# One attention and RWKV-style channel-mix block: row sums in the exp, a reordered layer norm, stores on another queue, and an add moved between engines

## The reference

```python
z = layernorm(x)
q, k, v = z @ Wq, z @ Wk, z @ Wv
att = softmax(einsum('bid,bkd->bik', q, k), axis=1)   # over i
x = x + tile(att @ v, (1, 1, 16))
z = layernorm(x)
z_prev = z shifted by one token, first row zero
xr = mu_r * z + (1 - mu_r) * z_prev
xk = mu_k * z + (1 - mu_k) * z_prev
r = sigmoid(xr @ W_r.T)
y = x + r * (square(relu(xk @ W_k.T)) @ W_v.T)
```

## Time and profile before

| | before |
|---|---|
| median of 2 runs | 833.14 us (832.54 to 833.75) |
| profiled execution, own time | 834.7 us |
| its span, slowest core (core 1) | 833.1 us |
| the next, core 7; fastest, core 5 | 832.4 us; 820.7 us |
| TensorE busy | 365.2 us, 44% |
| VectorE busy | 355.3 us, 43% |
| ScalarE busy | 238.2 us, 29% |
| GpSimd busy | 85.1 us, 10% |

### The profile page before, as it was taken

How to read it: one execution, slowest core, us unless ns; L and a number is a source line. 1 busy time by engine, 2 the same in 40 slices (tenths; PEclk the granted TensorE clock), 3 DMA queues, 4 the chain that set the end, 5 groups by cost and what they waited for, 6 DMA issues and landing times.

```text
span 833.1 us, 5659 instructions; the slowest of 8 cores (820.7 to 833.1 us)
## 1 busy us (share of the span) xinstructions
PE 365.2 (44%) x1392; PEld 125.8 (15%) x1392; DVE 355.3 (43%) x515; ACT 238.2 (29%) x356; POOL 85.1 (10%) x93
## 2 busy tenths in 40 slices
PE   0004000079465656565653000000439999986660
PEld 0001000034011111111112000000114444432220
DVE  4506152576325252525352586629940012233432
ACT  4104040400474747475750232200022233300000
POOL 3102011110002000000000011000000000044443
PEclk9999555589555565555555555555759999999896
DMA  9966958370101994000000014474000000044543
GB/s 228 294 109 174 212 146 250 90 151 1 31 8 18 165 208 127 1 0 0 1 0 1 4 29 155 169 168 81 6 0 1 1 0 1 12 165 152 172 182 126
DMA packets 76996, 75.82 MB, mean 91 GB/s; under 512 B 59427, under 2 KB 59443, under 8 KB 76900
## 3 DMA queue, kind: packets, MB, share of 16 engines
q0 software_dynamic: 13504, 32.32, 14.9%
q1 hardware_dynamic: 12516, 30.49, 11.2%
q10 hardware_dynamic: 50944, 12.65, 9.1%
HBM read 47.79 MB, written 21.56 MB: 83 GB/s over the span
## 4 chain that ended last, share of the span: by engine, by line
DMA 35%; PE 19%; DVE 19%; issue 12%; ACTq 6%; ACT 5%; POOL 2%; DVEq 1%; POOLq 0%; SPq 0%
DMA v_sb<-vdram 13%; DMA xst<-x_in 12%; PE ktp L918 6%; PE rps L878 6%; DMA zdram<-zst 5%; ACTq L334 4%; DVE ell L548 4%; DMA z1T<-z1dram 2%; DVE x1b L717 2%; DVE xk L857 2%; ACT p_sb L582 2%; POOL xst L996 2%; PE dpool L516 2%; DVE zst L375 2%; ACTq L808 1%
## 5 line engine op out<-in xcount | busy, mean ns | idle before, releaser
L516 PE MATMUL dpool<-qrep,krep 64*128 64x512 bf16 x256 | 108.1, 600 | 89.5 <-ACT p_sb L582 85.6
L878 PE MATMUL rps<-wrT,xr 128*128 128x512 bf16 x256 | 59.5, 397 | 158.3 <-DVE xr L848 138.1
L548 DVE TENSOR_REDUCE ell<-p_sb 128x1 f32<-128x4096 bf16 x16 | 70.7, 4419 | 125.8 <-ACT p_sb L582 125.8
L582 ACT ACTIVATE p_sb<-dpool,negm 128x1024 bf16<-128x1024 f32 x64 | 72.0, 1124 | 81.8 <-DVE negm L541 81.7
L415 PE MATMUL qk<-zT,wqk 128*128 128x512 bf16 x64 | 18.3, 438 | 162.6 <-DVE qrep L446 97.7
L975 PE MATMUL ops<-wvT,kaT 128*128 128x512 bf16 x256 | 62.4, 402 | 26.4 <-DVE tmp L1025 24.9
L586 ACT ACTIVATE p_sb<-dpool,negm 128x1024 bf16<-128x1024 f32 x64 | 72.3, 1129 | 0.0
L320 ACT ACTIVATE zst<-xst 128x1024 bf16<-128x1024 f32 x32 | 33.8, 1056 | 103.2 <-issue 91.1
L918 PE MATMUL ktp<-xk,wkT 128*128 128x512 bf16 x256 | 55.6, 379 | 1.7 <-ACT r_sb L891 1.3
L943 DVE TENSOR_TENSOR kaT<-kaT 128x512 bf16<-128x512 bf16 x32 | 13.6, 425 | 98.5 <-ACT kaT L934 98.4
L878 PEld LDWEIGHTS rps<-wrT,xr 128*128 128x128 bf16 x256 | 25.8, 101 | 191.6 <-issue 164.1
(11 more groups left out here) (85 smaller groups left out, 408.1 us busy)
## 6 DMA issues: line engine op xcount, KB each, us to landing
xst<-x_in SPq DMA_DIRECT2D x32, 512.0 KB, 10.1
xst<-x_in POOLq DMA_DIRECT2D x32, 512.0 KB, 5.2
zdram<-zst POOLq DMA_DIRECT2D x32, 256.0 KB, 9.3
y_out<-x2b SPq DMA_DIRECT2D x16, 512.0 KB, 3.6
z1dram<-z1b SPq DMA_DIRECT2D x16, 256.0 KB, 3.1
wrT<-wrT_in POOLq DMA_DIRECT2D x1, 2048.0 KB, 18.4
wkT<-wkT_in POOLq DMA_DIRECT2D x1, 2048.0 KB, 30.2
wvT<-wvT_in POOLq DMA_DIRECT2D x1, 2048.0 KB, 41.7
```

The source lines that it names most:

```text
L516: t.matmul(units[u][:, cc * 512:(cc + 1) * 512], krep[64 * a:64 * (a + 1), kt * 128:(kt + 1) * 128], qrep[64 * a:64 * (a + 1), c * 512:(c ...
L548: v.reduce_sum(ell[:, kt:kt + 1], p_sb[kt % 4][:, :], axis=AX.X).then_inc(SV, 1)
L582: sc.activation(p_sb[kt % 4][:, s * 1024:(s + 1) * 1024], units[u][:, :], AF.Exp, bias=negm[:, kt:kt + 1]).then_inc(SS, 1)
L878: ins = t.matmul(r_ps[t_ % 2][:, hh * 512:(hh + 1) * 512], xr[ct][:, t_ * 128:(t_ + 1) * 128], wrT[:, ct * C + hh * 512:ct * C + (hh + 1) ...
```

## The change

Four parts.

1. The exp of even k-tiles leaves the sums of its units in `ellp` too, in the other half of that buffer. VectorE's sum for an even k-tile goes over these four values instead of 4096.
2. The second layer norm's order on VectorE becomes that of the first: adds and sums of group 0, then finish and apply of g-1 and the adds and sums of g. `z1b` and its semaphores become eight. A new plan function `plan_ln_af2` counts in the new order.
3. The stores of the first layer norm move from GpSimd to SyncE. The store of tile i-8 stands behind the load of tile i, whose waits it uses; the last eight stores follow with waits of their own.
4. In the last stage GpSimd only loads. VectorE adds `out_tok` to `tmp32` between the product and the last add, which now waits for the load itself.

The core of the diff (left out are the new plan function, the counts that follow from it, the slot indices of z1b, and the waits for eight semaphores ahead of the transposes):

```diff
-        ZSs = [e(nc.semaphore(f"ZS{i}")) for i in range(4)]
+        ZSs = [e(nc.semaphore(f"ZS{i}")) for i in range(8)]
...
-        zs_f = lambda t: 16 * (t // 4 + 1)
+        zs_f = lambda t: 16 * (t // 8 + 1)
...
-        F_CNT, SV_Floop = plan_ln(TOWN, SV_TAIL, ("x1",))
+        F_CNT, SV_Floop = plan_ln_af2(TOWN, SV_TAIL)
...
                 sy.dma_start(out=xst[:, s * C:(s + 1) * C],
                              in_=x_in[i * 128:(i + 1) * 128, :]).then_inc(DSs[s], 16)
-
-        @block.gpsimd
-        def _(g):
-            for i in range(TT):
-                s = i % 8
-                g.wait_ge(SV, A_CNT[("apply", i)])
-                g.dma_start(out=zdram[i * 128:(i + 1) * 128, :],
-                            in_=zst[:, s * C:(s + 1) * C]).then_inc(ZAs[s], 16)
+                if i >= 8:
+                    j = i - 8
+                    sy.dma_start(out=zdram[j * 128:(j + 1) * 128, :],
+                                 in_=zst[:, (j % 8) * C:(j % 8 + 1) * C]).then_inc(ZAs[j % 8], 16)
+            for j in range(TT - 8, TT):
+                sy.wait_ge(SV, A_CNT[("apply", j)])
+                sy.dma_start(out=zdram[j * 128:(j + 1) * 128, :],
+                             in_=zst[:, (j % 8) * C:(j % 8 + 1) * C]).then_inc(ZAs[j % 8], 16)
...
                     v.wait_ge(SS, d_exp(kt, 3))
-                    if kt % 2 == 0:
-                        v.reduce_sum(ell[:, kt:kt + 1],
-                                     p_sb[kt % 4][:, :],
-                                     axis=AX.X).then_inc(SV, 1)
-                    else:
-                        v.reduce_sum(ell[:, kt:kt + 1],
-                                     ellp[:, 4:8],
-                                     axis=AX.X).then_inc(SV, 1)
+                    v.reduce_sum(ell[:, kt:kt + 1],
+                                 ellp[:, 4 * (kt % 2):4 * (kt % 2) + 4],
+                                 axis=AX.X).then_inc(SV, 1)
...
-                        if kt % 2 == 0:
-                            sc.activation(p_sb[kt % 4][:, s * 1024:(s + 1) * 1024],
-                                          units[u][:, :], AF.Exp,
-                                          bias=negm[:, kt:kt + 1]).then_inc(SS, 1)
-                        else:
...
+                        sc.activation(p_sb[kt % 4][:, s * 1024:(s + 1) * 1024],
+                                      units[u][:, :], AF.Exp,
+                                      bias=negm[:, kt:kt + 1],
+                                      accum_out=ellp[:, 4 * (kt % 2) + s:
+                                                     4 * (kt % 2) + s + 1]).then_inc(SS, 1)
...
-                  nc.sbuf_tensor("z1b", [128, 4 * C], BF16)]
+                  nc.sbuf_tensor("z1b", [128, 8 * C], BF16)]
...
-            for g in range(4):
+            for s in range(4):
+                f_x1_sum(v, s)
+            for g in range(1, 4):
+                emit_ln_fin(v, g - 1, F_CNT, f_square(4 * (g - 1) + 3),
+                            f_sqrt(g - 1))
+                f_apply_emit(v, g - 1)
                 for s in range(4):
                     f_x1_sum(v, g * 4 + s)
-                if g >= 1:
-                    emit_ln_fin(v, g - 1, F_CNT, f_square(4 * (g - 1) + 3),
-                                f_sqrt(g - 1))
-                    f_apply_emit(v, g - 1)
             emit_ln_fin(v, 3, F_CNT, f_square(15), f_sqrt(3))
             f_apply_emit(v, 3)
...
                 g.dma_start(out=xst[:, (t_ % 8) * C:(t_ % 8 + 1) * C],
                             in_=x_in[t_ * 128:(t_ + 1) * 128, :]).then_inc(FSs[t_ % 8], 16)
-                g.wait_ge(FSs[t_ % 8], fs_k(t_))
-                g.tensor_tensor(xst[:, (t_ % 8) * C:(t_ % 8 + 1) * C],
-                                xst[:, (t_ % 8) * C:(t_ % 8 + 1) * C],
-                                bass.AP(out_tok, t_ * D, [[TOWN * D, 128], [0, 16], [1, D]]),
-                                ALU.add).then_inc(SH, 1)
...
-                v.wait_ge(SH, t_ + 1)
                 v.wait_ge(SV, k_tmp(t_))
+                v.tensor_tensor(tmp32[:, (t_ % 2) * C:(t_ % 2 + 1) * C],
+                                tmp32[:, (t_ % 2) * C:(t_ % 2 + 1) * C],
+                                bass.AP(out_tok, t_ * D, [[TOWN * D, 128], [0, 16], [1, D]]),
+                                ALU.add).then_inc(SV, 1)
+                v.wait_ge(FSs[t_ % 8], fs_k(t_))
+                v.wait_ge(SV, k_mid(t_))
                 v.tensor_tensor(x2b[:, (t_ % 2) * C:(t_ % 2 + 1) * C],
                                 tmp32[:, (t_ % 2) * C:(t_ % 2 + 1) * C],
                                 xst[:, (t_ % 8) * C:(t_ % 8 + 1) * C], ALU.add).then_inc(SV, 1)
```

More of the change, by code:

```diff
@@ L239, in build_program, with plan_ln_af2 @@
         SS_TAIL = SS_F0 + 2
-        F_CNT, SV_Floop = plan_ln(TOWN, SV_TAIL, ("x1",))
+        def plan_ln_af2(n_tiles, sv0):
+            ng = n_tiles // 4
+            cnt = {}
+            sv = sv0
+            for s4 in range(4):
+                sv += 1
+                cnt[("x1", s4)] = sv
+                sv += 1
+                cnt[("sum", s4)] = sv
+            for g in range(1, ng + 1):
+                gm = g - 1
+                for op in ("smean", "svar", "msq", "varsub", "recip", "nmr"):
+                    sv += 1
+                    cnt[(op, gm)] = sv
+                for s4 in range(4):
+                    sv += 1
+                    cnt[("apply", 4 * gm + s4)] = sv
+                if g < ng:
+                    for s4 in range(4):
+                        i = 4 * g + s4
+                        sv += 1
+                        cnt[("x1", i)] = sv
+                        sv += 1
+                        cnt[("sum", i)] = sv
+            return cnt, sv
+        F_CNT, SV_Floop = plan_ln_af2(TOWN, SV_TAIL)
         f_square = lambda t: SS_TAIL + 5 * (t // 4) + (t % 4) + 1
@@ L804, in _ @@
             sc.wait_ge(SD, sd_zero1)
-            for s in range(4):
-                sc.wait_ge(ZSs[s], zs_f(4 + s))
+            for s in range(8):
+                sc.wait_ge(ZSs[s], 16)
             for ctn in range(CT):
```

22 lines of the change are left out of this document (9 added, 13 removed).

## The result

The changed kernel takes 732.62 us (median of 11 runs, 728.83 to 738.65), the kernel before 833.38 us in the runs beside it. The ratio is 0.8776 with a 95% interval of 0.8745 to 0.8808: 100.8 us less. The forecast was 727 us, from 716 to 745. The profiled execution took 732.77 us, its span 731.2. Any kernel of this program now and then runs in a slower state, in which the cores of one die show a lower granted clock; ratios and times here are of the other, fast executions.

What follows compares the result with a forecast made beforehand. The chain of waits, not a full engine, was taken to bound the kernel. -56.8 - 11.8 - 36.2 - 1.5 = -106.3 from the profiled 834.7 gave 728.4, less 1.6 to the runs' median: 727 us, range 716 to 745.

Steps and rivals of the forecast that it cites:

- Attention, -56.8 forecast: Attention: the long sum leaves the path of all 16 pairs, 3.55 us less per pair, -56.8 us.
- The pair built from pieces: Attention: the new pair's period, assembled from spacings in the trace, 3.59 us less than the old 13.95.
- The allowance for TensorE: Attention: a gain of 3.55 us a pair taken instead of 3.59, as TensorE's scores come close.
- Second layer norm, -11.8 forecast: Second layer norm: the new order ends VectorE's waits of 5.83, 4.65 and 1.66 us, less 0.3 for finishes.
- Last stage, -36.2 forecast: Last stage: without GpSimd's add a tile takes 3.85 us, the last x2b starts at 790.8 instead of 826.98.
- three paces: Last stage, per tile: VectorE's operations 3.78 us, TensorE's matmuls 3.61, the store's buffer round 3.79 at median landing.
- (a): Last stage: the store of y paces tiles as store and load start together; 4.85 a tile, +15, 742 us; chance 0.13.
- Stores of the first layer norm, -1.5 forecast: First layer norm: stores moved to SyncE's queue; only the last landing counts, late engines' amount stays fixed; -1.5 us.
- (c): First layer norm: the first quarter's stores come free near 41.5 us; -5.5 more, 721 us; chance 0.11.
- (b): Attention: TensorE's scores set the pair at 11.1 us; +11, 738 us; chance 0.10.
- (e): First layer norm: SyncE's queue finishes one transfer before the next begins; +146, 873 us; chance 0.01.
- (d): Last stage: TensorE falls to 1.2 GHz, a tile takes 7.2 us; +50, 777 us; chance 0.03.

Runs made afterwards that it cites:

- undo run: Attention: the changed kernel with the 4096-value sum put back, 799.37 us. Stores: the changed kernel with first layer norm stores back on GpSimd's queue, 729.76 us.
- e11_w_q2: The changed kernel with four x2b slots and GpSimd's six small weight loads held back until the third quarter's transposes have landed; 719.44 us, ratio 0.8611.

## Why the prediction was right

**Attention, -56.8 forecast, -58.2 measured.** The pair built from pieces was 10.36 us, taken as 10.40; it is 10.34. All steps hold: 7.64 for the eighth exp (7.63), 0.81 for the short chain (0.80), 0.54 to the exp. The allowance for TensorE was not needed. The undo run shows that the long sum was on the path of every pair. With 3.61 us instead of the 3.55 taken, 16 pairs give 57.8 of the 58.2. The transposes of `v_sb` stayed covered, as the unbroken period of 10.34 shows.

**Second layer norm, -11.8 forecast, -9.5 measured on the mean.** The waits for loads went as said. Two sizes were off. I had read the gain from core 1, whose stage of 67.7 us was the longest of the eight; the mean was 66.5, so 1.2 us of the difference is a choice of core. And the finishes now cost 0.24 + 0.24 + 0.23 + 0.50 = 1.2 us instead of the 0.3 in the sum, since each waits for a square that ends just behind the last sum.

**Last stage, -36.2 forecast, -31.3 measured.** This is the term that failed in size, and by more than the difference says: 60.4 us were forecast for the stage, from core 1's 96.6, and it takes 66.5 on the mean and 69.2 on the slowest core. Two of the three paces in it are right: VectorE's 3.78 us (3.79 measured) and TensorE behind it. The third was worked out from the median landing, (3.97 + 3.6) / 2 = 3.79, "a tie", and I then took 3.85. With a tie the median is the wrong number. The wait exists in those tiles whose store lands late, and a store that lands early gives nothing back, because VectorE's own three operations take 3.78. At 3.97 + L over two tiles a store above 3.6 us costs its excess, less what VectorE has lost to another wait since that store was issued. On core 3 eight stores were above 3.6, and five products waited, for 8.6 us. What changed against the earlier trace rows is the spread: over the eight cores 30 of 128 stores land in more than 4.5 us, before 2 did. The run with four slots takes the wait away and nothing else, and gets 59.5 us on every core, where 2.64 + 15 x 3.79 = 59.5 is VectorE's own work. The rival (a) had this mechanism, the store of y pacing tiles because loads and stores now go together, and its sign, idle time that ends on `y_out`, is there. At 4.85 a tile it overstated the size: 66.5 - 2.6 over 15 is 4.26.

**Stores of the first layer norm, -1.5 forecast, 0.0 measured.** Within what can be told, nothing. The forecast held that only the landing of the last store counts. In the fourth quarter that landing does come 1.5 us sooner behind the last apply, but the first exp hangs on the apply and not on the landing. The argument that a late engine has a fixed amount to move, whichever queue it stands in, is borne out by the undo run. In the changed kernel the same 7 us lie there, moved to the other queue (last columns: clock, DMA share, GB/s), as does the long landing of the first quarter's last store in the chain:

```profile
41.00:48.00 7.00, 0.00 (x0) 0.00 (x0) 0.00 (x0) 0.00 (x0) 0.00 (x0) 1.00 0.18 64
```

```profile
32.65 15.71 DMA zdram<-zst
...
81.46 8.96 DMA zdram<-zst
```

The window shows 18% against the 21% of the earlier trace rows, and the landing is 15.71 us after an issue 2.5 us later than in the earlier trace rows. "DMA: Bandwidth & Descriptors" of the Trainium skill, section "Issuing engines are not separate DMA queues", says that DMAs from different issuers share the same 16 DMA engines and interleave; the 18% and the 15.71 us agree with it. "SBUF — State Buffer" of the Trainium skill, section "SBUF: two separate sides", warns that GpSimd cannot write descriptors while VectorE runs a two-port mode. Here stores on GpSimd's queue cost nothing that could be measured in the kernel's time, 0.8753 against 0.8776; whether the 2.9 us landing of the last store on that queue, against 2.1, is this effect, no run here shows. The rival (c) was right that the small weight packets were behind the late engines and wrong in what cures it: not the other queue, but another time.

**The sum.** -106.3 forecast, -100.8 measured in the medians; the differences of the table add up to -101.8, and the mean span fell by 101.7. By the table the forecast was too good by 4.9 us in the last stage, 2.3 in the layer norm and 1.5 in the stores, 8.7 together. It was too modest by 1.4 in the attention, 0.9 in the three stages in between and 1.9 at the end of the span: 4.2, of which the last 1.9 were not thought of.

Part of the closeness is luck. The time is that of the slowest core, and that was core 1 before and core 3 after. From the one to the other the last stage gained only 27.4 us (96.6 to 69.2), and 4.9 us came from an earlier first exp (215.0 to 210.1), which on the mean of the cores did not move.

**The rivals.** (b), TensorE's scores at 11.1 us a pair, did not happen; nor did (e). (d), TensorE at 1.2 GHz in the last stage, happened in one tile of the slowest core, and in one and two tiles of cores 4 and 5. Three tiles behind a wait, and a window in the first of them (columns as in the earlier trace rows, ahead of the clock the busy times of PE, PEld, DVE, ACT and POOL):

```profile
686.21 13.44 PE L994 MATMUL ops<-wvT,kaT 128*128 128x512 bf16 x48 [3.18 <-DVE tmp L1039]
```

```profile
690.00:692.00 2.00, 2.00 (x6) 0.73 (x5) 1.90 (x2) 0.00 (x0) 0.00 (x0) 0.50 0.45 174
```

The first of these tiles took 6.53 us where the other fifteen took 3.6, and it cost VectorE the 0.54 us of tile 8. The wait of 3.18 us ahead of it goes back to a late store. In the kernel before, on core 1, three tiles behind waits took 5.3 us, so the argument from the one tile at 741.36 was weaker than it looked.

## What to carry to other kernels

When two rates tie, a wait that closes the ring with only two buffers lets late transfers cost their excess while early ones give nothing back, and the median duration does not show it: look at the longest landing and ask whether one more slot costs anything. A transfer that is slow because the engines are busy with small packets is not helped by another queue; it is helped by issuing the small packets when no one is waiting, and one must follow the time through to the next stage, since 7.8 us gained in one quarter were all gone by the fourth. When a forecast is made from the slowest core, its stages are that core's own: the next kernel's slowest core can be another. Where a wait recurs in a loop, build the new period from spacings seen in the trace; it came out within 0.02 us.

## What was not expected of the hardware

The small weight loads are short when little else runs and long beside other traffic. The first landed 19.4 us after its issue among the loads of the second quarter and 5.4 us after it when issued just ahead of them. How much they cost the others depends on when they run: 7.8 us in the first quarter, 6.5 in the second, and nothing clear of noise in the fourth (0.3), for the same 0.86 MB.

The granted clock in the record does not always tell TensorE's pace. Here are windows ahead of and in the projections, for e11_w_q2 and for the changed kernel (columns: PE, PEld, DVE, ACT, POOL busy, clock, DMA share, GB/s):

```profile
120.00:150.00 30.00, 0.00 (x0) 0.00 (x0) 4.55 (x11) 8.18 (x15) 4.43 (x6) 1.00 0.79 153
157.00:200.00 43.00, 41.48 (x192) 18.19 (x190) 30.14 (x46) 0.00 (x0) 0.00 (x0) 1.00 0.37 75
```

```profile
120.00:150.00 30.00, 0.00 (x0) 0.00 (x0) 7.72 (x11) 4.60 (x8) 0.00 (x0) 0.50 0.77 201
166.00:210.00 44.00, 37.42 (x166) 16.23 (x166) 25.76 (x39) 1.19 (x1) 0.00 (x0) 0.93 0.34 60
```

In the changed kernel TensorE did 32 projection matmuls from 62 us on, was recorded at 0.50 (1.2 GHz) while it then waited 95 us, and its mean over the rest of the projections was 0.93. In e11_w_q2 it had done no matmul before and was recorded at 1.00 (2.4 GHz) throughout. Yet its first eight matmuls were no faster. The first and a later group of eight on core 0, in e11_w_q2 and then in the changed kernel behind its long wait:

```profile
149.77 3.57 PE L444 MATMUL qk<-zT,wqk 128*128 128x512 bf16 x8 [149.77 <-DMA ident<-ident_in]
...
155.44 1.89 PE L444 MATMUL qk<-zT,wqk 128*128 128x512 bf16 x8
```

```profile
163.43 3.53 PE L443 MATMUL qk<-zT,wqk 128*128 128x512 bf16 x8 [94.14 <-DVE qrep L474]
166.79 1.89 PE L448 MATMUL qk<-zT,wkq 128*128 128x512 bf16 x8
```

On all eight cores of both kernels such a first eight takes 3.2 to 3.4 us from start to start, and a later one 1.72. The difference is where it stands. In the changed kernel the slow eight stand on the path, behind the copies that follow VectorE's last apply. In e11_w_q2 they run at 144 to 157 us, on every core before that apply has ended. The 1.65 us between the two are most of the 1.9 by which the first exp there comes sooner after the last apply (44.9 instead of 46.9). No run changed this by itself. It also means that this run's higher mean granted clock (0.795 against 0.721 on the slowest cores) is in part a clock recorded while TensorE did nothing.
